# A counting stage's one-hots: numbers from SBUF instead of PSUM, two pairs interleaved

## The chip, the cores and the metric

The kernel runs on one NeuronCore of a Trainium2 chip. The metric is the device time of one execution in microseconds, a median over several executions. The engines: PE (TensorE, matrix products), DVE (VectorE), ACT (ScalarE), POOL (GpSimd) and SP (SyncE, here a DMA queue). SBUF is the on-chip memory of 128 partitions, PSUM the memory into which PE writes.

## The reference, cut to what matters

Two layers of a graph network over 12,500 nodes with 64 features and 400,000 edges that are sorted by their target.

```
h = relu(layernorm(x))                                   # 12500 x 64
e = silu(layernorm(concat(h[src], edge_attr) @ W1 + b1)) # per edge
m = silu(e @ W2 + b2)
x = x + layernorm(silu(concat(segment_sum(m, dst), h) @ Wu + bu))
h = relu(layernorm(x))
g = h + segment_sum(h[src], dst)                         # per edge: a row, no weights
x = x + relu(g @ M1 + c1) @ M2 + c2
```

The second layer's sum over the edges is a product of a matrix of counts (how often does node s stand as a source of node d) with h. The first layer needs the messages themselves, one by one.

## The kernel before, in words

**Stages.** The setup (to about 198 us) normalises x, multiplies it with the upper part of W1 into a table `layer_rows` in HBM, one row per node, counts the edges of each node (`deg`), and writes a table of source keys. Its part `column_one_hots` (L554 to L564) builds one-hots by comparisons of bf16 numbers in SBUF, interleaved by two, and PE multiplies them (L684). Then comes the first layer's loop over the edges, to 4286 us; then the update of the nodes; then the second layer, in which PE multiplies stored counts (L1664) while 78 of the 391 blocks of edges are gathered as in the first layer; then the last products and the output.

**The first layer's loop.** The edges are cut into 391 blocks of 1024, and the loop has one step per block, written out for every engine in `step(e, j)`. It is a pipeline over steps: each stage of a block has a lag. For each block GpSimd issues 8 indirect gathers (`gather`, L730), each of 128 rows of the table, whose row numbers it takes from `idx` in SBUF. SP loads the edges' attributes. PE multiplies these (L743); VectorE adds both (`z_ready`, L1137), which is what waits for the gathers; four blocks at a time the sums of squares are reduced (L1119) and the inverse root is taken in a chain of 12 small instructions (L278 to L288); VectorE scales (L1159), PE transposes (L750), ScalarE takes the silu (L1081), PE multiplies (L756), ScalarE takes the silu (L766), PE transposes back (L761), ScalarE copies (L770). VectorE makes a one-hot of each edge's place in its window of 40 nodes (`one_hot`, L785) and PE sums with it (L775); VectorE adds the sums into `cT` (L818, L822). GpSimd may be 4 blocks ahead of `z_ready` (L961).

**The counting.** Woven into the same steps, the second layer's counts are made. There are 79 tiles of 128 target nodes, each with 64 slots for the sources of its nodes. A source is told by two keys, low (0 to 127) and high (up to 200 values). 8 slots ("pairs") make a unit; 632 units stand at a rate of 13 in 8 steps. GpSimd fetches a tile's keys (L953), VectorE masks the unused ones (L1174, L1178), PE turns them (L997), and ScalarE copies them as bf16 into `low_key` and `high_key` in SBUF (L1070, L1071). `count_hots` then makes the one-hots of a unit with two VectorE instructions, and `pairs` multiplies low with high, 8 products of 128 x 200 (L986); ScalarE copies these to `stage` (L1063), and SP writes them out (L938). A unit's one-hots have one of four slots, released when PE has multiplied (`c_use`).

The order on VectorE in each step is: the layer's work (`layer_step`), a mask, then the comparisons of one or two units. In the comparisons the first input is a row of numbers 0..127, or 1..200 with a gap, f32 in PSUM; they are copied there once from `iol` and `ioh`, the bf16 originals in SBUF, which hold each number twice side by side.

Of the kernel before, what the change touches and what calls it, by code (L numbers as in the profile page):

```python
# [16 lines left out]
def build_gnn(nc, x, src, dst, src_rows, dst_rows, dst_heads, head_cols, edge_quads, W1, b1, g1, be1, W2, b2, Wu, bu, gn, bn, M1, c1, M2, c2, out):  # L17
    f32, bf16, i32, i16 = mybir.dt.float32, mybir.dt.bfloat16, mybir.dt.int32, mybir.dt.int16
    ALU = mybir.AluOpType
# [15 lines left out]
    T = N // TP  # L35
# [19 lines left out]
    GP = 8  # L55
# [7 lines left out]
    with ctx:  # L63
        def sb(name, shape, dt=f32):
            return ctx.enter_context(nc.sbuf_tensor(name, shape, dt))
# [25 lines left out]
        def sem(name):  # L91
            return ctx.enter_context(nc.semaphore(name))
# [21 lines left out]
        iol = sb("iol", [128, 128, 2], bf16)  # L114
        ioh = sb("ioh", [128, 2 * T, 2], bf16)
# [40 lines left out]
        view, again = region("node_buffers", room)  # L156
# [19 lines left out]
        STAGES = 4  # L176
        stage = view([128, STAGES, 2 * GP * T], bf16)
        PAIR_SLOTS = 4
        low_hot = view([128, PAIR_SLOTS, GP, 128], bf16)
        high_hot = view([128, PAIR_SLOTS, GP, 2 * T], bf16)  # L180
        node_keys = view([128, 2, SLOTS, 2], bf16)
        low_key = view([128, 2, 64], bf16)
        high_key = view([128, 2, 64], bf16)
# [27 lines left out]
        view, again = region("edge_buffers", max(3 * F * T * 2, 3 * 4 * BLOCKS * BC + 1024))  # L211
# [20 lines left out]
        ps = ctx.enter_context(nc.psum_tensor("ps", [128, 8, 512], f32))  # L232
        zp, tp, mp, ag = ([ps[:, 2 * k + i, :] for i in range(2)] for k in range(4))
# [7 lines left out]
        def bcast(a, n):  # L241

            return a.unsqueeze(2).broadcast_to([a.shape[0], a.shape[1], n])

        def per_tile(a, n):

            return a.unsqueeze(1).broadcast_to([a.shape[0], n, a.shape[1]])

        NORM = 15
        def wait(eng, semaphore, value):  # L250

            if not isinstance(value, int) or value > 0:
                eng.wait_ge(semaphore, value)  # L253
# [485 lines left out]
        def edge_products(pe, j, o=None):  # L739

            o = zp[0] if o is None else o
            for k in range(QUADS):
                mm = pe.matmul(o[:, k * 4 * F:(k + 1) * 4 * F], ea[:, j, k, :], w1e[:, :], start=True, stop=True)  # L743
            return mm
# [85 lines left out]
        def lagged(e, j, lag):  # L830

            return (j - lag) % UN, e * DB + j - lag

        def rows_before(e, j):

            return 2 * e + j // UN

        def there(n):

            return not isinstance(n, int) or 0 <= n < BLOCKS  # L840
# [33 lines left out]
        g_num = sem("l0_numbers_ready")  # L874
# [5 lines left out]
        c_low = sem("stored_low_one_hots_ready")  # L880
        c_hot = sem("stored_pair_one_hots_ready")
        c_use = sem("stored_pairs_multiplied")
        c_copy = sem("stored_counts_staged")
        c_st = [sem(f"stored_counts_written{k}") for k in range(STAGES)]
        low_numbers = ps[:, 7, 128:256]
        high_numbers = ps[:, 7, 256:256 + 2 * T]
        UNITS = TILES * GPS
        FETCH, MASK, KEYS_TURN, HOTS, COUNT, STORE = 0, 4, 6, 8, 9, 13
        unit_step = [u * RATE[1] // RATE[0] for u in range(UNITS)]
# [3 lines left out]
        def units_before(step):  # L893

            return sum(k < step for k in unit_step)

        def tiles_before(step):

            return sum(k < step for k in tile_step)
# [26 lines left out]
        with nc.Block() as block:  # L926
# [40 lines left out]
            @block.tensor  # L967
            def _(pe):
                def edges(e, j):

                    s, n = lagged(e, j, 0)
                    if there(n):

                        wait(pe, g_ea[s], rows_before(e, j) * 16 + 16)
                        wait(pe, g_z, n)
                        edge_products(pe, s, zp[0]).then_inc(g_ep, 1)

                def pairs(u, part):

                    wait(pe, c_hot, u + 1)  # L980
                    wait(pe, c_copy, 2 * u + part)
                    if part == 0:
                        wait(pe, c_kc, 2 * tiles_before(unit_step[u] + COUNT - KEYS_TURN))
                    for i in range(4):
                        k = part * 4 + i
                        mm = pe.matmul(tp[i // 2][:, i % 2 * 2 * T:(i % 2 + 1) * 2 * T], low_hot[:, u % PAIR_SLOTS, k, :],  # L986
                                       high_hot[:, u % PAIR_SLOTS, k, :], start=True, stop=True)
                    mm.then_inc(c_use, 1)

                def turn_keys(b):  # L990

                    wait(pe, c_msk, b + 1)
                    wait(pe, c_copy, 2 * units_before(tile_step[b] + KEYS_TURN - COUNT + 1))
                    wait(pe, c_kc, 2 * b)
                    for k in range(2):
                        for h in range(2):
                            mm = pe.matmul(tp[k][h * 64:(h + 1) * 64, 4 * T:4 * T + 64], node_keys[:, b % 2, :, k],  # L997
                                           identb[:, h:128:2], start=True, stop=True)
                    mm.then_inc(c_kt, 1)

                def step(e, j):
                    s, n = lagged(e, j, WSUM)
                    if there(n):

                        wait(pe, g_msg, n + 1)
                        wait(pe, g_oh, n + 1)
                        wait(pe, g_add, n)
                        window_sums(pe, s, msg[:, s, :, :], ag[0]).then_inc(g_sum, 1)
                    edges(e, j + EARLY)
                    units = units_at(e, j, COUNT)  # L1010
                    for u in units[0:1]:
                        pairs(u, 0)
                    s, n = lagged(e, j, TURN)
                    if there(n):

                        wait(pe, g_n, n + 1)
                        wait(pe, g_h, n)
                        transposes(pe, s, zp[1]).then_inc(g_t, 1)
                    for u in units[0:1]:
                        pairs(u, 1)  # L1020
                    s, n = lagged(e, j, BACK)
                    if there(n):

                        wait(pe, g_mt, n + 1)
                        wait(pe, g_msg, n)
                        back_transposes(pe, (j - BACK) % 2).then_inc(g_bt, 1)
                    for u in units[1:2]:
                        pairs(u, 0)
                    s, n = lagged(e, j, SECOND)
                    if there(n):  # L1030

                        wait(pe, g_h, n + 1)
                        wait(pe, g_mt, n)
                        second_products(pe, s).then_inc(g_m, 1)
                    for u in units[1:2]:
                        pairs(u, 1)
                    b = tile_at(e, j, KEYS_TURN)
                    if b is not None:
                        turn_keys(b)
                with pe.If(flagged(pe) == 0):  # L1040
                    for j in range(EARLY):
                        edges(0, j)
                    rounds(step, WSUM)
# [68 lines left out]
            def _(v):  # L1112
# [57 lines left out]
                def mask(b):  # L1170
# [6 lines left out]
                    high = node_keys[:, b % 2, :, 1]  # L1177
                    v.tensor_tensor(high, high, slot_used[:, :], ALU.mult).then_inc(c_msk, 1)  # L1178

                def count_hots(u):  # L1180

                    b, at = u // GPS, slice(u % GPS * GP, (u % GPS + 1) * GP)
                    wait(v, c_kc, 2 * b + 2)
                    wait(v, c_use, 2 * (u - PAIR_SLOTS) + 2)
                    v.tensor_tensor(low_hot[:, u % PAIR_SLOTS, :, :], per_tile(low_numbers, GP), bcast(low_key[:, b % 2, at], 128),  # L1185
                                    ALU.is_equal).then_inc(c_low, 1)
                    v.tensor_tensor(high_hot[:, u % PAIR_SLOTS, :, :], per_tile(high_numbers, GP), bcast(high_key[:, b % 2, at], 2 * T),  # L1187
                                    ALU.is_equal).then_inc(c_hot, 1)

                def step(e, j):  # L1190
                    layer_step(e, j)
                    b = tile_at(e, j, MASK)
                    if b is not None:
                        mask(b)
                    for u in units_at(e, j, HOTS):
                        wait(v, g_num, 3)
                        count_hots(u)

                def layer_step(e, j):
# [22 lines left out]
                        sums_added(e, j)  # L1222
                with v.If(flagged(v) == 0):
                    v.tensor_copy(numbers, winf[:, :]).then_inc(g_num, 1)
                    v.tensor_copy(low_numbers, iol[:, :, 0]).then_inc(g_num, 1)
                    v.tensor_copy(high_numbers, ioh[:, :, 0]).then_inc(g_num, 1)
                    rounds(step, WADD)

        def general(layer, table):
# [645 lines left out]
```

## Time and profile before

| what | value |
|---|---|
| median of 3 runs | 5370.95 us (5370.26 to 5372.14) |
| the profiled execution's own time | 5364.65 us |
| its span, first to last instruction | 5362.9 us |
| busy: PE / VectorE / ScalarE / GpSimd | 3761 / 3428 / 2145 / 3722 us |
| first layer's loop | from 198 us to 4286 us |

A busy time adds up the engine's records; it doesn't count waits, register work or the issue of a DMA by SP. "PEld" is PE's loading of weights, beside its products. In the groups, L1185 is the low comparison and L1187 the high one. A name such as `node_buffers` is a region of SBUF with many tiles in it, and `ps` is PSUM.

### The profile page before, as it was taken

What the parts mean: (1) busy time and instruction counts of PE and PEld (TensorE: products, weight loads), DVE (VectorE), ACT (ScalarE), POOL (GpSimd) and SP (SyncE); (2) the same over time, 40 slices, a digit from 0 to 9 for tenths busy, and PEclk for the clock granted to TensorE, in tenths of its full rate; (3) what the DMA queues carried; (4) which work ended last, traced back from release to release, by engine and by line L of the source; (5) the groups of instructions that cost most, each with busy time, mean ns of one, the idle gap of its engine ahead of it and who ended that gap; (6) DMA issues with size and microseconds to landing.
All of it is one profiled execution on the core that took longest, in us unless ns stands there. A gap on an engine that the chain in (4) does not pass through costs nothing. (4 is left out here: it accounts for less than half of the span.)

```text
span 5362.9 us, 73932 instructions
## 1 busy us (share of the span) xinstructions
PE 3760.8 (70%) x24431; PEld 2852.1 (53%) x24431; DVE 3427.9 (64%) x5403; ACT 2145.2 (40%) x3187; POOL 3721.5 (69%) x3907
## 2 busy tenths in 40 slices
PE   5556666666666666666666666666666768999997
PEld 4434444444444444444444444444444547999994
DVE  5467777777777777777777777777777681111111
ACT  1135445544444444454444444544544530000003
POOL 2777777777777777777777777777777206777770
PEclk9568788888888888888888888878888858999999
DMA  3123333333333333333333333333333227999992
GB/s 98 49 82 106 104 104 109 106 104 100 111 104 104 103 105 104 104 109 106 104 101 108 106 104 102 107 103 104 110 105 104 82 62 300 352 354 352 351 354 59
DMA packets 361303, 729.02 MB, mean 136 GB/s; under 512 B 156402, under 2 KB 206834, under 8 KB 350306
## 3 DMA queue, kind: packets, MB, share of 16 engines
q1 hardware_dynamic: 238338, 598.51, 30.4%
q0 software_dynamic: 122592, 125.78, 11.8%
q8 instruction: 205, 3.36, 0.3%
q14 instruction: 168, 1.38, 0.1%
HBM read 450.70 MB, written 273.27 MB: 135 GB/s over the span
## 5 line engine op out<-in xcount | busy, mean ns | idle before, releaser
L730 POOL DMA_INDIRECT gat<-layer_rows,idx x3752 | 3548.2, 946 | 1145.3 <-issue 1142.0
L1063 ACT ACTIVATE node_buffers<-ps 128x800 bf16<-128x800 f32 x1264 | 1058.0, 837 | 1966.0 <-PE ps L986 1947.4
L775 PE MATMUL ps<-one_hots,edge_buffers 128*128 128x80 f32 x3128 | 576.4, 345 | 849.0 <-DVE cT L822 847.4
L1187 DVE TENSOR_TENSOR node_buffers<-ps,node_buffers 128x1600 bf16<-128x1600 f32 x632 | 1146.6, 1814 | 0.0
L775 PEld LDWEIGHTS ps<-one_hots,edge_buffers 128*128 128x128 f32 x3128 | 521.2, 252 | 998.7 <-issue 993.0
L986 PE MATMUL ps<-node_buffers 128*128 128x200 bf16 x5056 | 726.0, 272 | 243.8 <-ACT node_buffers L1063 128.2
L986 PEld LDWEIGHTS ps<-node_buffers 128*128 128x128 bf16 x5056 | 467.7, 106 | 651.8 <-issue 510.9
L1137 DVE TENSOR_TENSOR edge_buffers<-ps,gat 128x512 f32<-128x512 f32 x391 | 269.8, 690 | 808.7 <-issue 685.7
L1185 DVE TENSOR_TENSOR node_buffers<-ps,node_buffers 128x1024 bf16<-128x1024 f32 x632 | 770.7, 1219 | 9.6 <-issue 0.7
L1664 PE MATMUL ps<-edge_buffers,node_buffers 125*128 125x192 bf16 x7900 | 686.3, 248 | 6.1 <-PEq L1400 6.1
L1664 PEld LDWEIGHTS ps<-edge_buffers,node_buffers 125*128 125x128 bf16 x7900 | 665.7, 139 | 19.8 <-issue 19.8
L743 PE MATMUL ps<-w1e,edge_buffers 128*128 128x256 f32 x1564 | 597.2, 521 | 101.2 <-DVE edge_buffers L1137 97.2
L756 PE MATMUL ps<-edge_buffers,w2d 128*128 128x512 f32 x782 | 452.5, 662 | 173.1 <-ACT node_buffers L766 144.5
L818 DVE TENSOR_TENSOR cT<-cT,ps 64x40 f32 x469 | 86.0, 183 | 721.3 <-PE ps L775 580.0
L743 PEld LDWEIGHTS ps<-w1e,edge_buffers 128*128 128x128 f32 x1564 | 368.2, 260 | 153.1 <-issue 104.8
L750 PE MATMUL ps<-ident,node_buffers 128*128 128x128 f32 x1564 | 314.1, 339 | 13.6 <-ACT edge_buffers L1081 13.6
L1637 ACT ACTIVATE node_buffers<-ps 128x192 f32<-128x192 f32 x79 | 26.1, 330 | 717.0 <-PE ps L1664 717.0
L1081 ACT ACTIVATE edge_buffers<-ps,gcol 128x512 f32<-128x512 f32 x391 | 303.4, 776 | 10.4 <-PE ps L750 10.4
L1159 DVE TENSOR_TENSOR node_buffers<-edge_buffers,ps 128x512 f32<-128x512 f32 x391 | 265.9, 680 | 3.6 <-DVE ps L288 0.2
L766 ACT ACTIVATE node_buffers<-ps,b2col 128x512 f32<-128x512 f32 x391 | 266.4, 681 | 0.7 <-PE ps L756 0.5
L750 PEld LDWEIGHTS ps<-ident,node_buffers 128*128 128x128 f32 x1564 | 243.4, 183 | 20.5 <-issue 15.1
L756 PEld LDWEIGHTS ps<-edge_buffers,w2d 128*128 128x128 f32 x782 | 118.5, 191 | 253.3 <-issue 253.3
(186 smaller groups left out, 3197.4 us busy)
## 6 DMA issues: line engine op xcount, KB each, us to landing
stored_counts<-node_buffers SPq DMA_DIRECT2D x632, 400.0 KB
node_buffers<-stored_counts SPq DMA_DIRECT2D x79, 3200.0 KB
gat<-layer_rows,idx POOLq DMA_INDIRECT x3752
edge_buffers<-in_edge_quads SPq DMA_DIRECT2D x391, 128.0 KB, 3.1
node_buffers<-in_x SPq DMA_DIRECT2D x5, 625.0 KB
layer_rows<-node_buffers SPq DMA_DIRECT2D x25, 125.0 KB
residual_rows<-node_buffers SPq DMA_DIRECT2D x5, 625.0 KB
layer_rows<-node_buffers SPq DMA_DIRECT2D x5, 625.0 KB
```

The source lines that it names most:

```text
L730: pool.indirect_dma_start(out=gat[:, j, c, :], out_offset=None, in_=table[:, :], in_offset=bass.IndirectOffsetOnAxis(ap=idx[:, half, j, c: ...
L743: mm = pe.matmul(o[:, k * 4 * F:(k + 1) * 4 * F], ea[:, j, k, :], w1e[:, :], start=True, stop=True)
L750: mm = pe.transpose(o[:, k * 128:(k + 1) * 128], zn[:, j, 2 * k:2 * k + 2, :].rearrange("p c f -> p (c f)"), ident[:, :])
L756: return pe.matmul(mp[0][:, 0:PAIRS * 128], w2d[:, :], hT[:, j, :], start=True, stop=True)
L775: mm = pe.matmul(to[:, 0:2 * WIN], rows_of[:, 2 * k:2 * k + 2, :].rearrange("p c f -> p (c f)"), oh[:, j, 2 * k:2 * k + 2, :].rearrange("p ...
L986: mm = pe.matmul(tp[i // 2][:, i % 2 * 2 * T:(i % 2 + 1) * 2 * T], low_hot[:, u % PAIR_SLOTS, k, :], high_hot[:, u % PAIR_SLOTS, k, :], st ...
L1063: a.activation(stage[:, u % STAGES, part * GP * T:(part + 1) * GP * T].rearrange("p (b k) -> p b k", b=2), ps[:, 2:4, 0:4 * T], ACT.Copy). ...
L1081: a.activation(hT[:, s, :], zp[1][:, 0:PAIRS * 128], ACT.Silu, bias=gcol[:, 1:2], scale=gcol[:, 0:1]).then_inc(g_h, 1)
L1137: v.tensor_tensor(zb[:, j // UN % 2, s, :, :], zp[0][:, 0:BC * F].rearrange("p (c f) -> p c f", c=BC), gat[:, s, :, :], ALU.add).then_inc( ...
L1185: v.tensor_tensor(low_hot[:, u % PAIR_SLOTS, :, :], per_tile(low_numbers, GP), bcast(low_key[:, b % 2, at], 128), ALU.is_equal).then_inc(c ...
L1187: v.tensor_tensor(high_hot[:, u % PAIR_SLOTS, :, :], per_tile(high_numbers, GP), bcast(high_key[:, b % 2, at], 2 * T), ALU.is_equal).then_ ...
L1664: mm = pe.matmul(wide[d % 2], cnt[d % 3][0:TP, t:t + (GW - 1) * T + 1:T], hparts[:, t, :, :].rearrange("p k f -> p (k f)"), start=(t == 0) ...
```

## The change

The numbers are no longer copied to PSUM. The comparisons read `iol` and `ioh` (bf16, SBUF) as they are, each number twice in a row, and beside them the keys of two neighbouring pairs. For that the one-hots lie interleaved: for 4 couples of pairs, for each number, the two pairs' values side by side. PE therefore reads a pair's one-hots with a step of two elements. The number of VectorE's instructions, their elements and their order stay; two copies and one wait (for these copies) go.

```
-        low_hot = view([128, PAIR_SLOTS, GP, 128], bf16)
-        high_hot = view([128, PAIR_SLOTS, GP, 2 * T], bf16)
+        low_hot = view([128, PAIR_SLOTS, GP // 2, 128, 2], bf16)
+        high_hot = view([128, PAIR_SLOTS, GP // 2, 2 * T, 2], bf16)
...
-        low_numbers = ps[:, 7, 128:256]
-        high_numbers = ps[:, 7, 256:256 + 2 * T]
...
-                        mm = pe.matmul(tp[i // 2][:, i % 2 * 2 * T:(i % 2 + 1) * 2 * T], low_hot[:, u % PAIR_SLOTS, k, :],
-                                       high_hot[:, u % PAIR_SLOTS, k, :], start=True, stop=True)
+                        mm = pe.matmul(tp[i // 2][:, i % 2 * 2 * T:(i % 2 + 1) * 2 * T], low_hot[:, u % PAIR_SLOTS, k // 2, :, k % 2],
+                                       high_hot[:, u % PAIR_SLOTS, k // 2, :, k % 2], start=True, stop=True)
...
+                def spread(keys, b, at, n):
+
+                    return keys[:, b % 2, at].rearrange("p (a b) -> p a b", b=2).unsqueeze(2).broadcast_to([128, GP // 2, n, 2])
...
-                    v.tensor_tensor(low_hot[:, u % PAIR_SLOTS, :, :], per_tile(low_numbers, GP), bcast(low_key[:, b % 2, at], 128),
-                                    ALU.is_equal).then_inc(c_low, 1)
-                    v.tensor_tensor(high_hot[:, u % PAIR_SLOTS, :, :], per_tile(high_numbers, GP), bcast(high_key[:, b % 2, at], 2 * T),
-                                    ALU.is_equal).then_inc(c_hot, 1)
+                    v.tensor_tensor(low_hot[:, u % PAIR_SLOTS, :, :, :], iol[:, :, :].unsqueeze(1).broadcast_to([128, GP // 2, 128, 2]),
+                                    spread(low_key, b, at, 128), ALU.is_equal).then_inc(c_low, 1)
+                    v.tensor_tensor(high_hot[:, u % PAIR_SLOTS, :, :, :], ioh[:, :, :].unsqueeze(1).broadcast_to([128, GP // 2, 2 * T, 2]),
+                                    spread(high_key, b, at, 2 * T), ALU.is_equal).then_inc(c_hot, 1)
...
-                        wait(v, g_num, 3)
...
-                    v.tensor_copy(low_numbers, iol[:, :, 0]).then_inc(g_num, 1)
-                    v.tensor_copy(high_numbers, ioh[:, :, 0]).then_inc(g_num, 1)
```

## Rows read from the trace of the kernel before

**Rows 1.** The page's first part: busy time, share of the span, instructions.
```profile
PE 3760.8 (70%) x24431; PEld 2852.1 (53%) x24431; DVE 3427.9 (64%) x5403; ACT 2145.2 (40%) x3187; POOL 3721.5 (69%) x3907
```

**Rows 2.** By windows: stretch; busy us of PE, PEld, DVE, ACT, POOL; clock; DMA.
```profile
300.00:4200.00 3900.00, 2568.69 (x13561) 1806.09 (x13562) 2998.04 (x4520) 1903.87 (x2713) 2947.91 (x3124) 0.82 0.36 105
```

**Rows 3.** Waits of POOL from 1000 to 3500 us: total us, times, longest.
```profile
POOL gat L730 <- issue: 595.2, 1953, 0.3
POOL gat L730 <- PE ps L997: 0.6, 2, 0.3
```

**Rows 4.** The timeline of POOL: start, length, idle before.
```profile
2031.73 0.94 POOL L730 DMA_INDIRECT gat<-layer_rows,idx  x1 [0.30 <-issue]
2032.98 0.94 POOL L730 DMA_INDIRECT gat<-layer_rows,idx  x1 [0.30 <-issue]
2034.22 0.94 POOL L730 DMA_INDIRECT gat<-layer_rows,idx  x1 [0.30 <-issue]
```

**Rows 5.** The page's groups: busy us, mean ns, idle before.
```profile
L1187 DVE TENSOR_TENSOR node_buffers<-ps,node_buffers 128x1600 bf16<-128x1600 f32 x632 | 1146.6, 1814 | 0.0
...
L1185 DVE TENSOR_TENSOR node_buffers<-ps,node_buffers 128x1024 bf16<-128x1024 f32 x632 | 770.7, 1219 | 9.6 <-issue 0.7
```

**Rows 6.** The timeline of DVE, two units one after the other.
```profile
2031.01 1.81 DVE L1187 TENSOR_TENSOR node_buffers<-ps,node_buffers 128x1600 bf16<-128x1600 f32 x1
2032.74 1.22 DVE L1185 TENSOR_TENSOR node_buffers<-ps,node_buffers 128x1024 bf16<-128x1024 f32 x1
2033.87 1.81 DVE L1187 TENSOR_TENSOR node_buffers<-ps,node_buffers 128x1600 bf16<-128x1600 f32 x1
```

**Rows 7.** Single lines of the setup: ns min/median/max.
```profile
L558 DVE TENSOR_TENSOR node_buffers<-iol,edge_buffers x10: 1479/1646/1992, 116.4 to 186.0; 125x2560 bf16<-125x2560 bf16 x10
...
L560 DVE TENSOR_TENSOR node_buffers<-iol,edge_buffers x10: 1171/1674/2493, 118.1 to 187.4; 125x1960 bf16<-125x1960 bf16 x10
...
L441 POOL COPY cT<-node_buffers x25: 589/602/2846, 27.6 to 181.9; 128x500 f32<-128x500 f32 x25
```

**Rows 8.** The timeline of POOL and DVE in the second layer, three pairs.
```profile
4442.63 1.70 DVE L785 TENSOR_TENSOR one_hots<-winf,rel_all 128x320 f32<-128x320 bf16 x4 [7.60 <-PEq L1400]
...
4443.52 1.24 POOL L730 DMA_INDIRECT gat<-layer_rows,idx  x1 [2.11 <-ACT idx L798]
...
4470.14 0.48 DVE L785 TENSOR_TENSOR one_hots<-winf,rel_all 128x320 f32<-128x320 bf16 x1
...
4470.03 1.41 POOL L730 DMA_INDIRECT gat<-layer_rows,idx  x1 [0.30 <-issue]
...
4480.22 0.48 DVE L785 TENSOR_TENSOR one_hots<-winf,rel_all 128x320 f32<-128x320 bf16 x1
...
4480.48 1.04 POOL L730 DMA_INDIRECT gat<-layer_rows,idx  x1 [0.30 <-issue]
```

**Rows 9.** Groups of POOL from 4440 to 5240 us, the second layer.
```profile
L730 POOL DMA_INDIRECT gat<-layer_rows,idx x624 | 596.5, 956 | 192.0 <-issue 189.9 <-ACT idx L798 2.1
```

**Rows 10.** The timeline of the setup at 158 us.
```profile
158.01 1.49 DVE L482 TENSOR_TENSOR node_buffers<-node_buffers,stat 125x1280 f32<-125x1280 f32 x1
158.12 1.84 POOL L441 COPY cT<-node_buffers 128x500 f32<-128x500 f32 x1
```

**Rows 11.** The timeline where the first layer's gathers end and its loop drains.
```profile
4201.39 0.94 POOL L730 DMA_INDIRECT gat<-layer_rows,idx  x1 [0.30 <-issue]
...
4254.05 1.23 DVE L1185 TENSOR_TENSOR node_buffers<-ps,node_buffers 128x1024 bf16<-128x1024 f32 x1
...
4261.78 0.19 DVE L818 TENSOR_TENSOR cT<-cT,ps 64x40 f32 x1 [3.53 <-PE ps L775]
```

**Rows 12.** The timeline of PE: the setup's column products and a unit's.
```profile
152.36 1.10 PE L684 MATMUL ps<-node_buffers 125*128 125x98 bf16 x20
...
2000.47 0.51 PE L986 MATMUL ps<-node_buffers 128*128 128x200 bf16 x4
```

**Rows 13.** The timeline of DVE where the first gathered rows land.
```profile
211.54 0.69 DVE L1137 TENSOR_TENSOR edge_buffers<-ps,gat 128x512 f32<-128x512 f32 x1 [12.82 <-DMA gat<-layer_rows,idx]
```

## The prediction

> **What bounds the kernel now.** I read the busy line first [rows 1]: PE, VectorE and GpSimd are all busy for 64 to 70% of the span, which decides nothing, because the span has stages. So I cut it. In the stretch from 300 to 4200 us [rows 2], the first layer's edge loop with the counting woven in, GpSimd does 3124 instructions in 3900 us, one every 1.248 us. Its wait view [rows 3] shows why that is the bound: in 2500 us the 1953 gathers waited 595 us "for issue", never over 0.3 us at a time, and for no other engine in any amount (0.6 us). GpSimd walks from one indirect gather to the next: 0.94 us busy, 0.30 us between them, without a pause [rows 4]. One step of the loop is one block of edges, eight gathers, 9.99 us, and a keys' fetch every fifth step. 3128 gathers and 79 fetches by 1.248 us are 4002 us, from the first at about 199 us to the last, which begins at 4201.39 us [rows 11]. So nothing shortens this stage unless it shortens or packs the gathers, and whatever lengthens one gather lengthens the span by the same.
>
> VectorE is busy 2998 of those 3900 us [rows 2] and does not bound it.
>
> **The change, part by part.** A unit of counting is a low comparison (8 x 128 = 1024 elements) and a high one (8 x 200 = 1600); there are 632 units, 13 in 8 steps.
>
> *The comparisons themselves.* Now 1219 and 1814 ns [rows 5]; in the timeline each begins 0.08 us before its predecessor's record ends (1.81 us long, next start 1.73 us on) [rows 6]. The form that the change brings in already stands in the setup: bf16, both inputs in SBUF, interleaved by two, a broadcast in the middle. L558 takes 1479 ns at least for 2560 elements and L560 1171 ns for 1960 [rows 7]: 308 ns for 600 elements, 0.513 ns each and 165 ns fixed. That makes the low one 0.69 us and the high one 0.99 us. VectorE is relieved of 0.53 + 0.83 = 1.36 us per unit, 860 us in all. In the gather-bound loop this is worth 0, as the gathers hide it; if they didn't, it could be at most the 860 us.
>
> *What the comparisons do to the gathers.* This is the term that counts. Before, one input is PSUM. The gather that begins at 2031.73 us lies wholly under the high comparison of 2031.01 us and still takes 0.94 us [rows 4, 6]. After, both inputs are in SBUF, and the trace has that case in the second layer, where the same small one-hot (L785, 0.48 us) reads its numbers from SBUF. Three pairs [rows 8]. The comparison that begins at 4480.22 us is still running when a gather begins at 4480.48; the gather takes 1.04 instead of 0.94. The one of 4470.14 ends at 4470.62, 0.59 us after its gather began, and the gather takes 1.41, 0.47 more. In the group of four that begins at 4442.63 us, each follows the one before after 0.40 us (1.70 us for four records of 0.48), so the third runs from about 4443.45 to 4443.93; the gather of 4443.52 takes 1.24, 0.30 more. All three fit one rule: the gather needs something from SBUF 0.12 us after its record begins, and gets it when the comparison ends: delay = end of the comparison, less start of the gather, less 0.12 (0.22 - 0.12 = 0.10; 0.59 - 0.12 = 0.47; 0.41 - 0.12 = 0.29). The mean gather there is 956 ns instead of 944 [rows 9]: 624 x 12 ns over 78 comparisons, 0.1 us for each, so nearly each comparison does it. The next gather starts 0.30 us after the longer one's end, so the delay isn't won back. Where a GpSimd copy and a two-input VectorE instruction overlap in the setup it is alike: the copy of 158.12 us, under L482 of 158.01 us, takes 1.84 us [rows 10], and 0.60 us by its median [rows 7].
>
> The Trainium skill says this in "SBUF — State Buffer", section "Who interferes with whom": a VectorE instruction with two SBUF inputs contends with a GpSimd instruction that reads SBUF, not with one that only writes. The trace agrees, with 1.41 us against 0.94. The same section infers, though, that a tensor_tensor leaves descriptor generation alone; by that the term would be nothing, and it is a rival below.
>
> *Its size.* A gather is hit if it begins while a comparison runs, I take from 0.05 us after the comparison's start until 0.12 us before its end (one that begins just ahead of the comparison should have its read done). If the gathers' starts lie anywhere in their 1.248 us, the low comparison has a window of 0.69 - 0.17 = 0.52 us and costs 0.52 x 0.52 / 2 / 1.248 = 0.108 us on average; the high one a window of 0.82 us and 0.82 x 0.82 / 2.496 = 0.269 us. If the low one delays a gather to its end, the next begins 0.94 - 0.12 + 0.30 = 1.12 us later, when the high one has ended (0.91 us later), so the two cost together a little less than the sum: 0.01 us off, 0.367 us per unit. x 632 = 232 us. The starts are not really anywhere, as VectorE's turn in each step begins on the landing of the last gather. Laid over the recorded starts of all 632 pairs, with the new lengths, the windows give 221 us; by the place of a unit in the cycle of 13 the mean runs from 0.17 to 0.47 us. An example from the rows: the low comparison of 2032.74 would end at 2033.43, and the gather of 2032.98 would be held 0.33 us; that of 2034.22 would meet the end of the high one (2034.34) and lose nothing. I take 221 us. The ends: 0.17 us for every unit if the phases lock well, 107 us; 0.57 us if, as at 4470.03 us, a comparison that begins up to 0.11 us after the gather holds it too (windows 0.68 and 0.98 us, 0.185 + 0.385), 360 us.
>
> *The tail.* After the last gather the loop drains 15 steps, until 4286 us. VectorE is back to back until its last unit at 4254.05 us; from 4261.78 us it waits for PE [rows 11]. 11 units begin in this stretch: up to 11 x 1.36 = 15 us to win. But PE and ScalarE work through the same steps just behind it, so they take over as the bound: between 0 and -15, I take -7 us.
>
> *PE reads every second element.* L684 does this in the setup with 98 columns: 20 products in 1.10 us, 55 ns each; L986 now takes 0.51 us for 4 of 200 columns, some 125 ns each [rows 12]. Twice 55 is still no more than now. Even if each product took 55 ns longer, 13 a step would add 0.7 us to a PE that is busy 2569 of 3900 us [rows 2]: 0, and at most a few us in the tail.
>
> *Two copies into PSUM and a wait less.* VectorE then has 12.82 us idle until the first gather lands at 211.54 us [rows 13]: 0.
>
> **Sum.** The profiled execution took 5364.65 us (span 5362.9). 5364.65 + 221 - 7 = 5579 us. The median of the runs, 5370.95, lies 6 above it, so 5585 us for the median.
>
> **Rivals.** *The gathers don't notice, and the tail shortens.* Reason for: the skill's inference; two bf16 comparisons are read in a packed way that no gather in this trace has met; VectorE may keep off the moments that count. Against: the three pairs. Time 5371 - 7 = 5364, at best 5356. This is the case on the other side; it decides where a gather under a comparison still takes 0.94 us.
> *Low and high hold the gather together.* VectorE has the high comparison ready when the low one ends; if it keeps what the gather wants, the window is 1.60 - 0.17 = 1.43 us: 1.43 x 1.43 / 2.496 = 0.82 us per unit, 518 us, 5880 us. Against: in the group at 4442.63 us the fourth comparison followed at once, and the gather went ahead at the third's end.
> *The comparisons keep their old rate.* Then they hold SBUF for 1.22 and 1.81 us. Low: window 1.05, 0.44 us. High: window 1.64, longer than a period, so every time the first gather is held, 1.64 - 0.62 = 1.02 us. 1.46 x 632 = 920 us, 6290 us. Against: L558 and L560 have this very pattern.
>
> **How the numbers follow.** The forecast 0.85 (with its ends of 107 and 360 us: 5471 to 5724), gathers untouched 0.07, both together 0.05, old rate 0.03. The range 5470 to 5700 holds most of the first case. A measurement tells 0.2% (11 us) from no change. Faster than that needs rival one with the whole of the tail: 0.03. Within: 0.05. Slower: 0.92.
>
> **What the next profile would show.** L1185 near 0.69 and L1187 near 0.99 us; L730 in the first layer's stretch with a mean near 944 + 221,000 / 3128 = 1015 ns, its longest near 0.94 + 0.82 = 1.8 us, and gaps still 0.30 us; VectorE's busy time down by some 860 us; last gather near 4422 us; everything from the update stage on shifted and otherwise alike. I am wrong if the gathers stay at 944 ns, or if their sum grows but the gaps shrink by as much, or if some other engine appears among GpSimd's waits.

## The result and the profile after

The changed kernel takes 5580.14 us in the median of four runs (5570.98 to 5639.36), the kernel before 5371.34 us: 1.0412 times as long, with an interval of 1.034 to 1.0484. The forecast was 5585 us. The profiled execution took 5582.58 us, with a span of 5580.8 us. One of the four executions of e13 below took 9143.92 us for a reason that no row shows, and its ratio goes by the other three.

The busy line of the page:

```profile
PE 3823.1 (69%) x24431; PEld 2899.2 (52%) x24431; DVE 2544.6 (46%) x5401; ACT 2145.5 (38%) x3187; POOL 3942.8 (71%) x3907
```

Against [rows 1], VectorE has lost 883 us of work and GpSimd has gained 221 us, with the same 3907 instructions. The comparisons in the page's groups (mean ns, idle before), where L1187 is now the low and L1189 the high one:

```profile
L1189 DVE TENSOR_TENSOR node_buffers<-ioh,node_buffers 128x1600 bf16<-128x1600 bf16 x632 | 621.2, 983 | 0.0
...
L1187 DVE TENSOR_TENSOR node_buffers<-iol,node_buffers 128x1024 bf16<-128x1024 bf16 x632 | 431.0, 682 | 0.7 <-issue 0.7
```

They answer to [rows 5], 1814 and 1219 ns. The names of the inputs tell the memory: `ioh` and `iol` lie in SBUF. The gathers from 300 to 4400 us, first as one line (ns min/median/max), then as a group (mean ns, idle before):

```profile
L730 POOL DMA_INDIRECT gat<-layer_rows,idx x3034: 941/947/3352, 299.2 to 4399.5; - x190
```

```profile
L730 POOL DMA_INDIRECT gat<-layer_rows,idx x3034 | 3081.4, 1016 | 925.1 <-issue 923.3 <-PE ps L995 1.8
```

The median gather is as it was to 3 ns, the longest lasts 3.35 us, and the mean is 1016 ns. GpSimd's waits from 1000 to 3500 us answer to [rows 3] and are of the same kind, never over 0.3 us:

```profile
POOL gat L730 <- issue: 561.1, 1840, 0.3
```

So the stage is bound as before, by gathers one behind the other, of which some are longer. A ledger of the two profiled executions, from starts in their timelines:

| part | before | after | difference |
|---|---|---|---|
| to the first key fetch | 198.76 | 202.70 | +3.94 |
| from there to the start of the last gather of the first layer | 4002.63 | 4223.28 | +220.65 |
| from there to the end of the drain | 84.74 | 77.76 | -6.98 |
| the rest of the span | 1076.74 | 1077.07 | +0.33 |
| sum | | | +217.94 |

The times differ by 5582.58 - 5364.65 = 217.93 us. The drain's two ends, for the kernel before:

```profile
4286.13 0.28 DVE L1546 COPY node_buffers<-rows 1x256 f32<-1x256 f32 x1 [1.87 <-PEq L1339]
```

and for the changed kernel, with its last gather:

```profile
4425.98 0.95 POOL L730 DMA_INDIRECT gat<-layer_rows,idx  x1 [0.30 <-issue]
...
4503.74 0.28 DVE L1545 COPY node_buffers<-rows 1x256 f32<-1x256 f32 x1 [1.87 <-PEq L1338]
```

**What lengthens the gathers.** A gather is called held here when it takes longer than 944 ns because of a comparison that runs when it begins, and what it takes above 944 ns is its excess. Counted through the whole trace (gathers of the first layer's loop and key fetches together), the excess is 219 us. It has kinds. 358 gathers began while a low comparison ran (from 0.05 us after its start to 0.12 us before its end, the windows of the prediction) and were held to its end, 80 us in all; the expectations below say 354, which is the same count with another rounding at the windows' ends. 142 began under a high one and were held to its end, or 0.1 us beyond, 57 us. 35 took over 2.5 us, 72 us. The rest is 10 us. One step shows the first kind (timelines of VectorE and GpSimd: start, length):

```profile
2010.41 0.98 DVE L1189 TENSOR_TENSOR node_buffers<-ioh,node_buffers 128x1600 bf16<-128x1600 bf16 x1
2011.31 0.68 DVE L1187 TENSOR_TENSOR node_buffers<-iol,node_buffers 128x1024 bf16<-128x1024 bf16 x1
2011.91 0.98 DVE L1189 TENSOR_TENSOR node_buffers<-ioh,node_buffers 128x1600 bf16<-128x1600 bf16 x1
```

```profile
2011.02 1.19 POOL L730 DMA_INDIRECT gat<-layer_rows,idx  x1 [0.30 <-issue]
2012.52 1.20 POOL L730 DMA_INDIRECT gat<-layer_rows,idx  x1 [0.31 <-issue]
```

The first high comparison ends at 2011.39 us: 2011.39 - 2011.02 - 0.12 = 0.25, and 0.94 + 0.25 = 1.19. The second ends at 2012.89: 0.25 again. The second value isn't chance. A gather held to an end E is followed by the next at E + 0.82 + 0.30 = E + 1.12, and the next unit's comparison of the same kind ends at E + 1.50, so the hold is 1.50 - 1.12 - 0.12 = 0.26 us. 236 gathers have an excess between 0.23 and 0.28 us.

A gather that is held 0.1 us beyond the comparison:

```profile
2000.06 0.98 DVE L1189 TENSOR_TENSOR node_buffers<-ioh,node_buffers 128x1600 bf16<-128x1600 bf16 x1
2000.96 0.17 DVE L283 TENSOR_SCALAR st<-st 128x32 int32<-128x32 int32 x1
```

```profile
2000.33 1.63 POOL L730 DMA_INDIRECT gat<-layer_rows,idx  x1 [0.31 <-issue]
```

Here the hold of 0.69 us ends with L283 (2001.13 - 2000.33 - 0.12 = 0.68), a one-input instruction from SBUF to SBUF. And a long one:

```profile
914.80 0.98 DVE L1189 TENSOR_TENSOR node_buffers<-ioh,node_buffers 128x1600 bf16<-128x1600 bf16 x1
915.70 0.68 DVE L1187 TENSOR_TENSOR node_buffers<-iol,node_buffers 128x1024 bf16<-128x1024 bf16 x1
916.30 0.98 DVE L1189 TENSOR_TENSOR node_buffers<-ioh,node_buffers 128x1600 bf16<-128x1600 bf16 x1
917.20 0.17 DVE L283 TENSOR_SCALAR st<-st 128x32 int32<-128x32 int32 x1
```

```profile
915.31 2.89 POOL L730 DMA_INDIRECT gat<-layer_rows,idx  x1 [0.30 <-issue]
918.50 0.94 POOL L730 DMA_INDIRECT gat<-layer_rows,idx  x1 [0.30 <-issue]
```

The gather began under a high comparison and was let in neither at that one's end nor at the next two's, but after L283: 917.37 - 915.31 - 0.12 = 1.94, and 0.94 + 1.94 = 2.88.

### The profile page after: what moved, and what is told of

Read it like the earlier page. It is cut to its first block and busy times, and to the rows that moved or that the text cites. A ratio compares the mean times of both kernels' runs of the same rounds, so it can differ in the third digit from the quotient of the medians.

```text
span 5580.8 us, 73926 instructions
## 1 busy us (share of the span) xinstructions
PE 3823.1 (69%) x24431; PEld 2899.2 (52%) x24431; DVE 2544.6 (46%) x5401; ACT 2145.5 (38%) x3187; POOL 3942.8 (71%) x3907
## 5 line engine op out<-in xcount | busy, mean ns | idle before, releaser
L730 POOL DMA_INDIRECT gat<-layer_rows,idx x3752 | 3768.1, 1004 | 1145.9 <-issue 1141.9
L775 PE MATMUL ps<-one_hots,edge_buffers 128*128 128x80 f32 x3128 | 596.3, 353 | 990.4 <-DVE cT L822 990.1
L775 PEld LDWEIGHTS ps<-one_hots,edge_buffers 128*128 128x128 f32 x3128 | 538.5, 259 | 1135.3 <-issue 1129.7
L984 PE MATMUL ps<-node_buffers 128*128 128x200 bf16 x5056 | 745.8, 275 | 246.5 <-ACT node_buffers L1061 144.5
L743 PE MATMUL ps<-w1e,edge_buffers 128*128 128x256 f32 x1564 | 630.5, 545 | 104.6 <-DVE edge_buffers L1135 100.5
L1189 DVE TENSOR_TENSOR node_buffers<-ioh,node_buffers 128x1600 bf16<-128x1600 bf16 x632 | 621.2, 983 | 0.0
L743 PEld LDWEIGHTS ps<-w1e,edge_buffers 128*128 128x128 f32 x1564 | 388.2, 274 | 161.5 <-issue 107.9
L1187 DVE TENSOR_TENSOR node_buffers<-iol,node_buffers 128x1024 bf16<-128x1024 bf16 x632 | 431.0, 682 | 0.7 <-issue 0.7
L750 PE MATMUL ps<-ident,node_buffers 128*128 128x128 f32 x1564 | 305.0, 330 | 21.2 <-ACT edge_buffers L1079 21.2
L761 PE MATMUL ps<-ident,node_buffers 128*128 128x128 f32 x1564 | 253.0, 286 | 0.0
```

The lines of the kernel that those rows point to most:

```text
L730: pool.indirect_dma_start(out=gat[:, j, c, :], out_offset=None, in_=table[:, :], in_offset=bass.IndirectOffsetOnAxis(ap=idx[:, half, j, c: ...
L750: mm = pe.transpose(o[:, k * 128:(k + 1) * 128], zn[:, j, 2 * k:2 * k + 2, :].rearrange("p c f -> p (c f)"), ident[:, :])
L775: mm = pe.matmul(to[:, 0:2 * WIN], rows_of[:, 2 * k:2 * k + 2, :].rearrange("p c f -> p (c f)"), oh[:, j, 2 * k:2 * k + 2, :].rearrange("p ...
L1187: v.tensor_tensor(low_hot[:, u % PAIR_SLOTS, :, :, :], iol[:, :, :].unsqueeze(1).broadcast_to([128, GP // 2, 128, 2]), spread(low_key, b, ...
L1189: v.tensor_tensor(high_hot[:, u % PAIR_SLOTS, :, :, :], ioh[:, :, :].unsqueeze(1).broadcast_to([128, GP // 2, 2 * T, 2]), spread(high_key, ...
```

## The experiments

Of 8 steps of the loop, 5 hold two units of counting and 3 hold one. A "second unit" is the later of two in a step (243 of the 632); all others are "first units". The edits are shown cut to what matters.

**e1: the layout alone.** Interleaved one-hots and PE's step of two, with the numbers f32 in PSUM.

```
-  iol[:, :, :].unsqueeze(1).broadcast_to([128, GP // 2, 128, 2])
+  low_numbers.unsqueeze(1).unsqueeze(3).broadcast_to([128, GP // 2, 128, 2])   # f32, PSUM; the high one alike
```

> The change's interleaved layout and PE's reading with a step of two stay, but the numbers are f32 in PSUM again, so each comparison has one SBUF input and its old length (1.22 and 1.81 us). My theory (two SBUF inputs hold up the gather's read): gathers at 944 ns, 5371 us, within 8 of before. Rival (PE's stepped reads or the layout cost something on the path): 5400 us or more, PE's products of a unit over 0.55 us for four.

5366.69 us against 5365.39 us, ratio 1.0006 (0.9996 to 1.0015). Comparisons of 1220 and 1815 ns. PE's products take 276 ns each by the page's mean, before 272:

```profile
L986 PE MATMUL ps<-node_buffers 128*128 128x200 bf16 x5056 | 749.0, 276 | 256.0 <-ACT node_buffers L1063 151.3
```

The layout and the stepped reads cost nothing that can be measured. Its drain took 83.1 us with comparisons of the old length, before 84.7: so much is scatter.

**e2 and e16: all in bf16, the numbers in PSUM.** This takes the second SBUF input away and leaves the packed pace.

```
+  low_numbers = ps[:, 7, 128:256].bitcast(bf16).rearrange("p (k e) -> p k e", e=2)
+  v.tensor_copy(ps[:, 7, 128:256], iol[:, :, :].rearrange("p k e -> p (k e)").bitcast(f32))    # once; 4-byte words
-  iol[:, :, :].unsqueeze(1).broadcast_to(...)
+  low_numbers.unsqueeze(1).broadcast_to(...)                                                   # the high one alike
```

> As the changed kernel, interleaved and all in bf16, but the numbers are read from PSUM (bf16 pairs, copied there once as 4-byte words). My theory, if the comparisons keep the packed rate (0.68 and 0.98 us): gathers at 944 ns, no lengthened ones, the drain after the last gather 7 us shorter, 5364 us. If the rate falls to 1.22 and 1.81 us: 5371. Rival (it is the packed rate, not the second SBUF input, that keeps the gather waiting): lengthened gathers as in the changed kernel, 5580 us.

> The version with bf16 numbers in PSUM once more, with five rounds, as it is the one that may beat both kernels. The first time it was 6 us below the kernel before. Theory (the drain after the last gather is shorter, as VectorE bounds it, and nothing else changes): 4 to 8 us faster than the kernel before, 0.999 of it. If it was chance: 1.000.

5359.15 us against 5365.39 (0.999, 0.998 to 0.9999) and 5359.16 against 5365.37 (0.9988, 0.9979 to 0.9997). The page of e2:

```profile
L1191 DVE TENSOR_TENSOR node_buffers<-ps,node_buffers 128x1600 bf16<-128x1600 bf16 x632 | 619.8, 981 | 0.0
L1189 DVE TENSOR_TENSOR node_buffers<-ps,node_buffers 128x1024 bf16<-128x1024 bf16 x632 | 433.7, 686 | 9.6 <-issue 0.7
```

Its gathers from 300 to 4190 us:

```profile
L730 POOL DMA_INDIRECT gat<-layer_rows,idx x3041: 940/944/1019, 299.3 to 4189.6; - x191
```

The comparisons are as fast as in the changed kernel, the gathers as undisturbed as before. So it is the second SBUF input and not the packed pace that holds the gathers. From the last gather's start to the end of the drain it takes 79.5 us in e2 and 78.0 in e16, before 84.7: that is about the gain. This version is 6 us faster than the kernel before, which is 0.1%, and both intervals end just below 1; it is some 220 us faster than the changed kernel.

**e3: the low comparison alone from SBUF.** The high one reads f32 numbers in PSUM, as in e1.

> Only the low comparison reads its numbers from SBUF (0.68 us), the high one from PSUM as before. In the changed kernel the low ones held 354 gathers for 80 us in all, none beyond the low one's end. My theory: 60 to 110 us more than before, gathers of at most 1.5 us, 5430 to 5480 us. Rival (the delay comes mostly from the pair standing together): under 30 us more.

5401.52 us against 5365.39 (1.0067, 1.005 to 1.0084): 36 us more, below my 60 to 110 and above the rival's "under 30". The excess of its gathers is 42 us. None is over 1.46 us:

```profile
L730 POOL DMA_INDIRECT gat<-layer_rows,idx x3007: 940/944/1459, 299.7 to 4189.7; - x188
```

All 189 held gathers fell into the low comparison of the first unit of a step; the 243 second units held none. An average over phases doesn't see that.

**e4: the high comparison alone from SBUF.** The low one reads f32 numbers in PSUM.

> Only the high comparison reads its numbers from SBUF (0.98 us), the low one from PSUM. In the changed kernel gathers begun under a high one cost 122 us, 65 of them in 32 gathers that were held through the whole next unit. My theory: these long holds need a next comparison with two SBUF inputs right behind, so none is over 0.94 + 0.82 us here; 60 to 170 us more than before, 5430 to 5540 us. Rival (a high one can keep the gather out beyond its end by itself): gathers of over 2.5 us remain.

5634.47 us against 5365.39 (1.0501, 1.0483 to 1.0518). This is 269 us more, and more than the whole change costs, though it does less. My expectation of at most 170 us was wrong; that no gather is over 0.94 + 0.82 us came out:

```profile
L730 POOL DMA_INDIRECT gat<-layer_rows,idx x2836: 940/944/1766, 299.0 to 4188.1; - x190
```

What happened stands in one step of its timelines:

```profile
2009.60 0.98 DVE L1191 TENSOR_TENSOR node_buffers<-ioh,node_buffers 128x1600 bf16<-128x1600 bf16 x1
2010.50 1.22 DVE L1189 TENSOR_TENSOR node_buffers<-ps,node_buffers 128x1024 bf16<-128x1024 f32 x1
2011.63 0.98 DVE L1191 TENSOR_TENSOR node_buffers<-ioh,node_buffers 128x1600 bf16<-128x1600 bf16 x1
```

```profile
2009.66 1.74 POOL L730 DMA_INDIRECT gat<-layer_rows,idx  x1 [0.30 <-issue]
2011.70 1.73 POOL L730 DMA_INDIRECT gat<-layer_rows,idx  x1 [0.30 <-issue]
```

The first high comparison holds a gather to E = 2010.58. The next gather begins at E + 1.12 = 2011.70; the second high one, behind a low one of 1.22 us, at E + 1.05 = 2011.63, just ahead of it, and holds it for nearly its whole length. In second units 239 gathers were held (0.78 us by the median, 175 us in all), in first units 265 (0.36 us, 105 us). A hold sets the phase of the next gather, and where the next comparison begins just ahead of that phase, the worst case becomes the rule.

**e13 (and e9): e4 with two tiny copies more.** If that is so, a delay of 0.16 us should free the second units.

```
+  if u % 13 in (1, 3, 6, 8, 11):              # second units of a step, ahead of the high comparison
+      for k in range(2):
+          v.tensor_copy(ps[:, 7, 480 + (2 * u + k) % 32:481 + (2 * u + k) % 32], shift[:, :])
```

> The kernel with the high comparison alone in SBUF and the second units' moved by two tiny copies, once more, since the chip of the first time was slow for another reason (the kernel before took 7797 us there, and GpSimd waited for others). Where the kernel before takes 5365 us: theory of phases 5450 to 5540 us, rival 5634 or a little more.

5496.97 us against 5362.58 us (1.0247, 1.0227 to 1.0268). Against e4, the same kernel with 480-odd instructions less on VectorE, this is 137 us faster. Second units held 49 gathers, 32 us, in place of 239 and 175 us; first units 273 and 107 us, about as in e4. The starts in the two traces show the shift itself: in e4, 181 gathers began 0.07 or 0.08 us after a second unit's high comparison and were held; in e13, 183 began 0.05 or 0.06 us ahead of one, and none was held. The phases are shown to set the size.

**e15: both from SBUF, not packed.** The kernel before, with its layout, and the numbers read from `iol` and `ioh` with a step of two.

```
-  per_tile(low_numbers, GP)
+  per_tile(iol[:, :, 0], GP)          # the high one alike
```

> The kernel before with one change: both comparisons read their numbers as bf16 from SBUF, every second element, not interleaved, so with two SBUF inputs but (I expect) the old lengths of 1.22 and 1.81 us. Theory (two SBUF inputs hold the gather, packed or not, to the comparison's end): a first unit costs some 0.44 + 0.49 us, the second one's high comparison begins at E + 1.06 just ahead of the gather of E + 1.12 and holds it 1.6 us; some 1.2 us per unit, 770 us, plus long holds: 6000 to 6400 us. Rival (only packed comparisons hold gathers): 5365 us.

6161.14 us against 5365.37 (1.1483, 1.1462 to 1.1504). The page and the gathers' line:

```profile
L1185 DVE TENSOR_TENSOR node_buffers<-ioh,node_buffers 128x1600 bf16<-128x1600 bf16 x632 | 1148.3, 1817 | 0.0
...
L1183 DVE TENSOR_TENSOR node_buffers<-iol,node_buffers 128x1024 bf16<-128x1024 bf16 x632 | 768.4, 1216 | 0.7 <-issue 0.7
```

```profile
L730 POOL DMA_INDIRECT gat<-layer_rows,idx x2527: 940/944/2603, 298.6 to 4188.9; - x195
```

With the comparisons as long as before, and only the memory of the numbers and their type (bf16) changed, the kernel is 796 us slower; the gathers' excess is 792 us. The type isn't the cause, as e2 has bf16 numbers in PSUM and no holds. Packing the comparisons is thus what keeps the change's loss at 209 us: it shortens the holds. The line above ends at 4189 us, the loop only at 4996; in the rest of it stand the two longest gathers:

```profile
4830.48 5.47 POOL L730 DMA_INDIRECT gat<-layer_rows,idx  x1 [0.30 <-issue]
```

It was held over the high comparison it began under and the whole next unit. Only these two of the 240 gathers that began under a high comparison with the next unit's behind it were held so.

**e14 (and e11): the changed kernel with one tiny instruction ahead of each unit.**

```
+  v.tensor_copy(ps[:, 7, 480 + u % 16:481 + u % 16], shift[:, :])    # ahead of the low comparison
```

> The changed kernel with one tiny one-input instruction ahead of each unit, once more, for the same reason. On the slow chip no gather was over 2.5 us here, but 29 were held for the rest of a low comparison and the whole high one behind it. Where the kernel before takes 5365 us: if those stay some 30 at 1.1 us, and the second units' holds grow by 0.1 us, 5540 to 5570 us; 5580 or more if the tiny instruction does nothing for the sum.

5657.22 us against 5362.58 (1.057, 1.0532 to 1.0609), 87 us above my 5540 to 5570, and 77 us more than the changed kernel; the gathers' excess is 294 us against 219. The longest gather is 2.37 us:

```profile
L730 POOL DMA_INDIRECT gat<-layer_rows,idx x2827: 940/944/2366, 299.1 to 4188.5; - x189
```

No gather is held over two units any more. But 98 gathers that began under a low comparison were now held through the high one behind it (1.08 us each on average, 105 us), which in the changed kernel none of 358 was. So in these runs a long hold goes over two-input instructions one behind the other (e3 and e4, where every other comparison has one SBUF input, have none) and ends with the last of them or with L283 behind it, but whether a gather is let in at the seam between two of them depends on something that these runs don't show.

**Four runs on a slower chip: e9, e10, e11, e12.** On it the kernel before took 7796.97 us. The changed kernel (e12) waited there for other things than gathers, as GpSimd's waits from 2000 to 4000 us show; the kernel before has no profile from this chip.

```profile
POOL node_buffers L951 <- PE ps L995: 450.1, 28, 29.4
POOL gat L730 <- issue: 323.6, 1058, 1.3
POOL gat L730 <- DVE edge_buffers L1135: 68.4, 9, 13.5
```

The core moved 71 GB/s from 300 to 4150 us against 99 in the changed kernel's first profile, at a mean granted clock of 0.70 against 0.81 (stretch; elapsed; busy us of PE, PEld, DVE, ACT, POOL; clock; DMA share; GB/s, here of e12):

```profile
300.00:4150.00 3850.00, 1715.61 (x9112) 1184.88 (x9112) 1441.25 (x3044) 1278.72 (x1824) 2123.55 (x2112) 0.70 0.25 71
```

In the second layer it moved some 245 GB/s, where the changed kernel's first profile moved some 352.

> As the kernel with the high comparison alone reading SBUF, with two tiny VectorE copies (one SBUF number to PSUM, about 0.16 us together) put ahead of the high comparison of the second unit of a step. In the kernel without them, 239 of the second units' high comparisons held a gather, 0.78 us by the median, because of a lock of phases: a gather held to a high comparison's end E is followed by the next at E + 1.12 us, and the second unit's high comparison begins at E + 1.06, just ahead of it. Theory of phases: 0.16 us later it begins behind the gather, and most of these 175 us go; adding work to VectorE makes this kernel 100 to 190 us faster, 5450 to 5540 us. Rival (the delays come from the share of time in which a comparison runs, whatever the phases): 5634 us or a little more.

> The changed kernel with the high comparison of a unit ahead of its low one. In the changed kernel a gather held by the low one always got in at its end although the high one was next, while a gather held by a high one with the next unit's low one behind it was in 32 of 75 cases held through that whole unit. If the border between units makes the long holds, gathers held by a low one that ends a unit now show them (over 1.5 us beyond). If it is the pair high, low, they now come within a unit and are frequent: more than 5580. Rule alone, without long holds: 5500 to 5560 us.

> The changed kernel with one tiny VectorE instruction (one SBUF number copied to PSUM) ahead of each unit's two comparisons. Theory: the long holds need two-input instructions back to back over the units' border; with one input in between they vanish (65 to 72 us), while the second unit's phase moves by some 0.1 us and its holds grow from 0.25 to 0.35 us (some 15 us): 5520 to 5550 us. Rival (long holds have another cause, the queue of waiting instructions as such): gathers of over 2.5 us remain and 5580 us or more.

> The changed kernel unchanged, on the same chip as the others, for a second profile. 5571 to 5640 us as before; where the number of gathers over 2.5 us (35 in the first profile, 72 us) differs, the time should differ by about 2.1 us for each.

Their times, 7602.18, 7509.97, 7532.33 and 7530.66 us, say nothing on those expectations: gathers did not bound the loop there. So what e12 was to test, whether the time goes with the number of gathers over 2.5 us, stays untested. All four are 2.5 to 3.8% faster than the kernel before on that chip (the changed kernel 0.9667, 0.9619 to 0.9716). So on this chip the change wins. With gathers in the shade, VectorE's shorter comparisons may be what counts: e9, where only the high one is shorter, gains least. This wasn't tested. The holds are seen there too: e12's gathers have an excess of 193 us, with 32 over 2.5 us (71 us).

e10 puts the high comparison of each unit first (the two calls change places). 289 gathers were held by a high one and let in at its end, though a low one followed, and only 7 took over 2.5 us. All 7 began under the low one that ends a unit, out of 12 that had the next unit right behind. By e10 alone the long hold goes with the border between units and not with the kinds; e14, with its long holds inside units, says that the border isn't needed either.

## Why the prediction was right

*The bound.* It held: waits of GpSimd "for issue", 0.3 us at most, before and after, and +220.65 of the +217.94 us lie between the first fetch and the last gather.

*The lengths of the comparisons.* Forecast 0.69 and 0.99 us, measured 0.682 and 0.983. VectorE lost 883 us of work, against 860; none of it came back in the loop. That this work is worth nothing there is shown by e2, which does the same and gains 6 us.

*The cause.* Two SBUF inputs, shown from both sides: e2 takes the second input away and keeps the pace, and the holds go; e15 keeps the old pace and adds the second input, and they come, 792 us of them. The rule read from three pairs, "held to the comparison's end, less 0.12 us", fits 482 of the 532 gathers that the windows name in the changed kernel to within 0.025 us.

The Trainium skill's "SBUF — State Buffer", section "Who interferes with whom", infers that a tensor_tensor spares descriptor generation. By that alone these gathers would stay at 0.94 us, and one took 2.89. The trace agrees with the section's rule on a GpSimd instruction that reads SBUF; a gather takes its row numbers from there. Whether it is that read that waits or the making of the descriptors, no run here tells apart.

*The size.* 221 us forecast, 219 us of excess. The number was right, and its make-up was not. The same windows laid over the changed kernel's own starts give 152 us, since holds move the gathers to where the next comparison catches them late; and the long holds that I had as a rival of their own, with 0.05, occur in 35 places and bring 72 us. I had forecast that no gather takes over 1.8 us; the longest took 3.35. The two errors cancelled, and that the total came out within 2 us is luck. e3 (42 us of excess, where uniform phases give 0.108 x 632 = 68) and e4 (279, where they give 0.269 x 632 = 170) show how far off an average over phases can be. My ends of 107 and 360 us were the honest part of that step, but the upper one rests on one pair that the loop doesn't repeat: I let a comparison hold a gather that began up to 0.11 us ahead of it, and in e13 none of the 190 gathers that began up to 0.1 us ahead of a second unit's high comparison was held. The gather of 4470.03 us, which was, stays unexplained.

*The drain.* -7 us forecast, -6.98 measured, and -5 to -7 in e2 and e16. I had only halved a range of 0 to 15, so the exact hit is luck too; e1 shows 1.6 us of scatter in this part. *PE's stepped reads and the two copies:* 0 and 0, shown by e1 (1.0006). The 3.94 us by which the first fetch came later lie in the setup, and e1, e3 and e16, which keep the two copies, have 198 to 202 us there too: scatter.

*The rivals.* "The gathers don't notice": fell. "Low and high hold together": it happens, in 35 cases and over two units. "Old rate": fell by the lengths; e15 shows what it would have cost, 6161 us, where I had 6290; its excess of 792 us stands against the 920 of the windows.

**Open:** what decides whether a held gather is let in between two two-input instructions; why the changed kernel's four executions lie 68 us apart, where the kernel before's lie 2 us apart; and why the change is 3.3% faster on the slower chip.

## What to carry to other kernels

When GpSimd issues gathers back to back and is the bound, look at VectorE's input memories before its busy time: here a comparison with two SBUF inputs held the gather that began under it at least until it ended (excess 219 us, unpacked 792), and one of the inputs in PSUM avoided it and cost nothing, with bf16 numbers at the packed pace too (e2). Where engines are locked in a cycle, don't average over phases: follow one hold to the next start and see where it falls, because two tiny instructions ahead of some comparisons were worth 137 us here. And check which engine is the bound on the machine at hand: where GpSimd wasn't, the same change gained 3.3%.

## What the runs showed of the hardware that was not expected

- A VectorE comparison with one bf16 input in PSUM and one in SBUF, and a bf16 output, runs as fast as with both in SBUF: 686 and 981 ns against 682 and 983 (e2 and the changed kernel), 1220 and 1815 with f32 numbers in PSUM (e1).
- A held gather isn't always let in between two VectorE instructions that follow one another: 32 of the 75 that began under a high comparison with the next unit's behind it waited for that whole unit (2.0 us on average), while all 358 under a low one got in at its end; with one tiny instruction ahead of the low one, 98 no longer did (e14).
- A short one-input instruction from SBUF to SBUF on int32 (L283, 0.17 us) can lengthen a hold by 0.1 us when it stands right behind the comparison: so it went in the changed kernel for 20 of the 50 gathers that began under such a high comparison.
- A gather that begins up to 0.1 us ahead of a comparison with two SBUF inputs goes ahead unhindered: all 190 ahead of a second unit's high comparison in e13 took 0.95 us at most. One in the kernel before, at 4470.03 us, was held all the same.
